# Four weight loads moved up in SyncE's queue, and the second context's split moved ahead of a small transpose's reading

## The chip, the cores and the metric

The kernel runs on one core of a Trainium2 chip. The metric is device microseconds for one execution of the whole program, lower is better. TensorE (PE) multiplies, VectorE (DVE), ScalarE (ACT) and GpSimd (POOL) do the elementwise work, and SyncE (SP) issues all of this kernel's DMAs from one queue. Each engine runs its own instructions in the order in which they were written, and waits on semaphores for the others.

## The reference, cut to what matters

Two cross-attention layers in sequence over 32 batches, 112 queries of 320 channels, 375 context rows of 512, 20 heads of 16. Both layers attend to the same context.

```python
# layer 0: text rows 0..76, image rows 77..374
q = heads(x @ Wq.T)
out  = attend(q, heads(text @ Wk.T), heads(text @ Wv.T))
out += attend(q, heads(ip @ Wk_ip.T), heads(ip @ Wv_ip.T))
x = out @ Wo.T + bo + x
# layer 1: text rows 0..370, image rows 371..374
q = heads(x @ W_q)
probs = softmax(q k_text / 4)
qsem = l2norm(probs @ text_ehs); sem = qsem . l2norm(ip_ehs)
probs_ip = softmax(q k_ip / 4 + 0.5 * sem) * spatial_mask
x = (probs @ v_text + probs_ip @ v_ip) @ W_out + b_out + x
```

## The kernel before, in words

The order of all work is one list of stages, written by hand in `stage_order`. Each engine has a function (`tensor`, `vector`, `scalar`, `gpsimd`, `sync`) that walks the list and issues its own part of each stage; so moving one line of `stage_order` moves work in the queues of all the engines that take part in that stage, and of no others. Stages of 32 batches follow one another with the next batch's projections mixed into the current one's attention; a batch takes some 78 us, and only the first two batches have a start of their own. The change lies in that start.

The start, in the order of the list (b is the batch, l the layer, t text, None a tile that is shared by both layers):

- A context (512 x 375) is loaded by `("ctx", b)` and split by `("split", b)` into a rounded part `ch` (four ACT copies) and a rest `cl` (four POOL subtractions). Context 0 is loaded into `pvt`, context 1 into `w2both`, which the raw weights use before it.
- `keys(b, l, m)` makes one tile of keys: PE multiplies into a bank R, ACT rounds into `kst`, DVE subtracts, ACT or DVE rounds the rest, POOL subtracts once more, and SP stores the three parts in HBM (`k_split`). `keys(0, 0, 0)` is the first image key tile; its store is line 1362. There are five staging buffers at first: tile (0, 1, 1), the eighth, takes the buffer of tile (0, None, 0), the sixth, and its copy on ACT waits until that tile's store has landed.
- `key_weights 1` rounds and splits the layer-1 key weights `wk1` (tile V in the trace, as they are loaded into the space of V1): ACT writes `wkh`, DVE `wkl`. `keys(0, 1, m)` needs both.
- `("load", 2)` are four DMAs of SP: `wk1` (512 KB), `wvip1`, `wv0` and `wvip0` (640 KB each). The third waits for the split of the first key weights, the fourth for the end of `image_keys` on PE.
- `k_stack` and `q_stack` read the stored keys and queries back from HBM in the layout of the attention (tiles Ks and Qs). Part 0 of the keys and all queries are needed for the first `s_max`.
- `image_values`, `weights 2` and `text_values(0)` come between: ACT and DVE make norms and split `wv0`, then PE makes the values of batch 0.
- `s_max` are eight rounds of PE products whose maxima DVE takes. `m_T` turns them back with one transpose of PE (line 692), ACT copies it into `mrem` and `ms`, POOL makes three parts (`m_split`), and SP sends them in six DMAs into rows of Qs (line 1397). These are "the first maxima's turning back". The attention's `scores` wait for these DMAs.
- `("split", 1)` stood behind this. PE's `keys(1, 0, 0)` and `keys(1, 0, 1)`, which need it, stand ahead of the first `scores`.

PE's list around the end of the start is thus: `s_max` x8, `m_T`, two key tiles of batch 1, `scores` 0.

Of the kernel before, what the change touches and what calls it, by code (L numbers as in the profile page):

```python
# [52 lines left out]
def stage_order():  # L53
    o = Order()
# [3 lines left out]
    def in_bank(what, signal, value):  # L58
        o.share("R", 3, what, signal, value)

    def flush():
        now = later[:]
        later.clear()
        for stage in now:
            o.add(*stage)

    def keys(b, l, m):
        o.add("k", b, l, m)
        in_bank(("k", b, l, m), "k_rem", o.at("k", b, l, m))
        o.share("rem", 2, ("k", b, l, m), "k_low", o.at("k", b, l, m))  # L70
# [158 lines left out]
    def take(pieces, n):  # L229
        for _ in range(n):  # L230
            next(pieces, None)
# [11 lines left out]
    o.add("image_keys")  # L243
    for m in range(3):
        in_bank(("image_keys", m), "kip_rem", m + 1)
    keys(0, "t", 1)
    keys(0, 0, 1)
    keys(0, "t", 2)
# [1 line left out]
    keys(0, None, 0)  # L250
    queries(0, 0)
    o.add("key_weights", 1)
    o.add("load", 2)
    o.add("k_stack", 0, 0, 0)
    o.add("k_stack", 0, 0, 1)
    o.add("q_stack", 0, 0)
# [20 lines left out]
    rows0 = maxima(0, 0, lambda: take(start, 1))  # L277
    take(start, 99)
    flush()
    take(rows0, 9)  # L280
    o.add("split", 1)
    o.add("weights", 1)
    o.add("weights_done")
    rows1 = iter(())
# [97 lines left out]
def xattn_two_layers(nc, a, out):  # L382
# [3 lines left out]
    with ctx:  # L386
# [6 lines left out]
        def sem(name):  # L393
# [121 lines left out]
                                             "ones_rows", "wvip0", "wo0", "wq1", "wo1", "wv1", "small")}  # L515

        o = stage_order()
        at, slot = o.at, o.slot

# [976 lines left out]
```

## Time and profile before

| | us |
|---|---|
| median of 3 runs | 2602.32 (2602.14 to 2607.59) |
| the profiled execution | 2602.31 |
| its span from first to last instruction | 2600.5 |
| PE busy | 2466.5 (95%) |
| DVE busy | 1640.2 (63%) |
| ACT busy | 1233.1 (47%) |
| POOL busy | 767.3 (30%) |
| mean granted clock of TensorE | 0.984 |

The busy time is from the profile's page; PE being busy does not mean that it works at its peak. The timeline lists instructions in order of time; the waits tell what ended the idle time of each engine; the DMA view gives the time from a DMA's issue to its landing.

### The profile page before, as it was taken

To read this page: it belongs to the slowest core of one execution; us is meant where nothing else is said; L and a number is where in the kernel's file an instruction comes from. 1 tells how busy PE (TensorE), PEld (TensorE's weight loads), DVE (VectorE), ACT (ScalarE), POOL (GpSimd) and SP (SyncE) were. 2 spreads that over 40 slices of the span, in tenths; PEclk is the share of its full clock that TensorE was granted. 3 is DMA by queue.
4 is the path that set the end of the run, shared out by engine and by line. 5 is a ranking of instruction groups with operands and counts; after the bars stand their busy time and mean duration, and the time that the engine had idled before them with its cause. 6 is when DMAs were issued, how large, how long until landed. Compare 5 with 4: busy or idle time off the path is not lost.

```text
span 2600.5 us, 64042 instructions
## 1 busy us (share of the span) xinstructions
PE 2466.5 (95%) x26280; PEld 2120.9 (82%) x26280; DVE 1640.2 (63%) x3210; ACT 1233.1 (47%) x2305; POOL 767.3 (30%) x999
## 2 busy tenths in 40 slices
PE   4799999999999999999999999999999999999996
PEld 4688888888888888888888888888888888888874
DVE  2356676566676566676656676656676656667655
ACT  2344444554444554444554444554444554444543
POOL 2122323322333332332332332332332332333222
PEclk8899999999999999999999999999999999999997
DMA  7664767656677656677655577745677755567730
GB/s 184 119 98 80 105 96 105 86 91 93 89 95 105 98 84 89 89 95 114 89 87 88 86 108 100 100 75 92 95 94 104 94 85 90 85 93 98 89 38 7
DMA packets 493225, 241.46 MB, mean 93 GB/s; under 512 B 259627, under 2 KB 492923, under 8 KB 492924
## 3 DMA queue, kind: packets, MB, share of 16 engines
q1 hardware_dynamic: 492934, 237.37, 61.7%
q8 instruction: 208, 3.41, 0.7%
q14 instruction: 83, 0.68, 0.1%
HBM read 171.35 MB, written 64.59 MB: 91 GB/s over the span
## 4 chain that ended last, share of the span: by engine, by line
PE 78%; DVE 17%; issue 2%; ACT 1%; DMA 1%; SPq 1%; POOL 0%; DVEq 0%; ACTq 0%; POOLq 0%
PE ST L701 7%; DVE w L838 6%; PE PN L718 5%; PE R L745 5%; PE R L643 5%; PE R L657 4%; PE R L656 4%; PE R L594 4%; DVE m L922 4%; PE R L595 4%; PE PN L763 3%; PE R L659 3%; PE R L802 3%; PE R L597 3%; DVE w L835 3%; PE ST L683 2%
## 5 line engine op out<-in xcount | busy, mean ns | idle before, releaser
L1141 ACT ACTIVATE p<-ST 128x1344 f32<-128x1344 f32 x320 | 413.8, 1293 | 113.1 <-PE ST L704 108.7
L1271 POOL TENSOR_TENSOR w<-w 128x448 f32<-128x448 f32 (+1 forms) x256 | 331.0, 1293 | 424.9 <-DVE w L835 406.7
L838 DVE SCALAR_TENSOR_TENSOR w<-p,pr 128x1344 f32<-128x1344 f32 x160 | 296.7, 1854 | 174.7 <-ACT pr L1156 161.5
L835 DVE TENSOR_TENSOR rem<-R,kst 128x298 f32<-128x298 f32 (+2 forms) x181 | 89.9, 497 | 441.4 <-ACT kst L1035 441.4
L745 PE MATMUL R<-pr,Gh 128*128 128x448 f32 (+1 forms) x960 | 366.7, 382 | 0.0
L835 DVE TENSOR_TENSOR w<-R,w 128x448 f32<-128x448 f32 (+1 forms) x480 | 281.5, 620 | 70.5 <-PE R L750 60.1
L656 PE MATMUL R<-wvh,ch 128*128 128x320 f32 (+3 forms) x896 | 301.9, 337 | 3.7 <-DVE wvl L835 3.7
L1204 POOL TENSOR_TENSOR kst<-rem,kst 128x298 bf16<-128x298 f32 (+2 forms) x181 | 149.2, 824 | 480.4 <-ACT kst L1035 260.2
L657 PE MATMUL R<-wvh,cl 128*128 128x320 f32 (+3 forms) x896 | 279.1, 311 | 0.0
L594 PE MATMUL R<-ch,wkh 128*128 128x298 f32 (+1 forms) x640 | 217.2, 339 | 27.1 <-DVE wkl L835 21.7
L701 PE MATMUL ST<-Qs,Ks 100*128 100x112 bf16 (+1 forms) x3520 | 229.8, 214 | 13.1 <-DMA Qs<-ms 5.2
L701 PEld LDWEIGHTS ST<-Qs,Ks 100*128 100x128 bf16 (+1 forms) x3520 | 184.7, 98 | 65.9 <-issue 34.8
L1035 ACT ACTIVATE pvt<-PN 128x112 f32<-128x112 f32 (+1 forms) x320 | 98.0, 306 | 250.2 <-PE PN L767 193.4
L659 PE MATMUL R<-wvl,ch 128*128 128x320 f32 (+3 forms) x672 | 209.2, 311 | 0.0
L1156 ACT ACTIVATE pr<-ST 128x1344 fp32r<-128x1344 f32 x160 | 204.9, 1281 | 0.0
L595 PE MATMUL R<-cl,wkh 128*128 128x298 f32 (+1 forms) x640 | 202.1, 316 | 0.0
L745 PEld LDWEIGHTS R<-pr,Gh 128*128 128x128 f32 (+1 forms) x960 | 176.5, 184 | 22.6 <-issue 6.2
L748 PE MATMUL R<-pr,Gl 128*115 128x448 f32 (+1 forms) x480 | 176.3, 367 | 0.0
L750 PE MATMUL R<-pr,Gl 128*128 128x448 f32 (+1 forms) x480 | 175.8, 366 | 0.0
L926 DVE TENSOR_REDUCE m<-ST 112x3 f32<-112x1113 f32 x128 | 167.9, 1312 | 7.2 <-PE ST L685 7.2
L1035 ACT ACTIVATE V<-R 128x320 f32<-128x320 f32 (+2 forms) x160 | 67.5, 437 | 218.6 <-PE R L660 218.6
L656 PEld LDWEIGHTS R<-wvh,ch 128*128 128x128 f32 (+3 forms) x896 | 162.5, 181 | 9.0 <-issue 4.1
(189 smaller groups left out, 5825.6 us busy)
## 6 DMA issues: line engine op xcount, KB each, us to landing
Ks<-k_split SPq DMA_DIRECT2D x384, 140.6 KB, 6.0
Ks<-k_split SPq DMA_DIRECT2D x384, 93.8 KB, 8.4
Qs<-q_split SPq DMA_DIRECT2D x384, 70.0 KB, 8.7
w<-in_ctxT SPq DMA_DIRECT2D x31, 750.0 KB, 5.9
k_split<-kst SPq DMA_DIRECT2D x64, 281.2 KB, 3.5
k_split<-kst SPq DMA_DIRECT2D x63, 223.5 KB, 2.7
q_split<-qst SPq DMA_DIRECT2D x128, 84.0 KB, 2.7
k_split<-kst SPq DMA_DIRECT2D x64, 111.8 KB, 2.5
```

Of the source, the lines that this page charges most:

```text
L594: e.matmul(r[:, 0:t1 - t0], wh[:, k, c0:c0 + 128], h[:, k, t0:t1], start=k == 0, stop=False)
L595: e.matmul(r[:, 0:t1 - t0], wh[:, k, c0:c0 + 128], lo[:, k, t0:t1], start=False, stop=False)
L656: e.matmul(r[0:n, 0:C], h[:, k, :], wh[:, k, :], start=k == 0, stop=False)
L657: e.matmul(r[0:n, 0:C], lo[:, k, :], wh[:, k, :], start=False, stop=False)
L659: e.matmul(r[0:n, 0:C], h[:, k, :], wl[:, k, :], start=False, stop=False)
L701: e.matmul(ST[:, u, S * h:S * h + S], Ks[l][0:m, GH * g + h, 128 * u:128 * u + 128], Qs[l][0:m, GH * g + h, :], start=True, stop=True)
L745: e.matmul(r[0:nj, 0:QW], Gh[0:ROWS[u], q:q + nj], x[0:ROWS[u], QW * u:QW * u + QW], start=u == 0, stop=False)
L835: return e.tensor_tensor(to, x, y, op)
L838: return e.scalar_tensor_tensor(out=to, in0=x, scalar=s, in1=y, op0=op0, op1=op1)
L1141: e.activation(p32[i][:].rearrange("p (u q) -> p u q", u=3), st, ACT.Exp).then_inc(p_whole, 1)
L1156: e.activation(pr[n % 2][:].rearrange("p (u q) -> p u q", u=3), ST[:, :, 0:QW], ACT.Exp).then_inc(p_round, 1)
L1271: e.tensor_tensor(first, first, w2[n % 2][0:ROWS[j], QW * j:QW * j + QW], ALU.add).then_inc(ns_added, 1)
```

## The change

In `stage_order`, `("load", 2)` moves from behind `key_weights 1` to directly behind the stage `image_keys`. On SP, the only engine with a part in it, the four loads then stand behind the store of the first image key tile. And `("split", 1)` moves ahead of the remaining steps of `rows0` (`m_T` and `m_split`).

```diff
     for m in range(3):
         in_bank(("image_keys", m), "kip_rem", m + 1)
+    o.add("load", 2)
     keys(0, "t", 1)
...
     o.add("key_weights", 1)
-    o.add("load", 2)
     o.add("k_stack", 0, 0, 0)
...
     flush()
+    o.add("split", 1)
     take(rows0, 9)
-    o.add("split", 1)
     o.add("weights", 1)
```

SP's queue at the start. Each row is one DMA, written tile<-source tile; V is `wk1`'s place, p_1, w and p_0 those of the other three weights. Both pieces, where the loads stand now and where they stood:

```order
 L1362 DMA k_split<-kst 128x3x298
+L1286 DMA V<-in_wk 128x4x256
+L1286 DMA p_1<-in_wvip 128x4x320
+L1286 DMA w<-in_wv 128x4x320
+L1286 DMA p_0<-in_wvip 128x4x320
 L1357 DMA k_split<-pvt 128x3x77 x4
 L1362 DMA k_split<-pvt 128x3x298
```

```order
 L1379 DMA q_split<-qst 128x3x112 x2
 L1379 DMA q_split<-qst 64x3x112
-L1286 DMA V<-in_wk 128x4x256
-L1286 DMA p_1<-in_wvip 128x4x320
-L1286 DMA w<-in_wv 128x4x320
-L1286 DMA p_0<-in_wvip 128x4x320
 L1372 DMA Ks<-k_split 16x12x375 x6
 L1372 DMA Ks<-k_split 16x8x375 x6
```

They have moved past 19 DMAs: 15 stores of keys (lines 1357 and 1362), the load of the next text context (tx), and the three stores of the queries.

ACT's queue around the turning back (V is a copy of batch 0's values, `ch` the rounded context 1):

```order
 L1035 ACTIVATE V<-R 119x20x16
-L1035 ACTIVATE mrem<-R 40x112
-L1035 ACTIVATE ms<-R 40x112
-L1035 ACTIVATE ch<-w 128x375 x4
+L1035 ACTIVATE ch<-w 128x375 x4
+L1035 ACTIVATE mrem<-R 40x112
+L1035 ACTIVATE ms<-R 40x112
 L1035 ACTIVATE wvh<-p_1 128x1280
```

POOL's queue at the same place:

```order
-L1204 TENSOR_TENSOR mrem<-mrem,ms 40x112
-L1260 CAST ms<-mrem 40x112
-L1204 TENSOR_TENSOR ms<-mrem,ms 40x112
-L1204 TENSOR_TENSOR cl<-w,ch 128x375 x4
+L1204 TENSOR_TENSOR cl<-w,ch 128x375 x4
+L1204 TENSOR_TENSOR mrem<-mrem,ms 40x112
+L1260 CAST ms<-mrem 40x112
+L1204 TENSOR_TENSOR ms<-mrem,ms 40x112
 L1228 MEMSET V 128x60
```

The rows of the split and of the turning back have changed places on both engines. PE and DVE have the same instructions in the same order as before.

## Rows read from the trace of the kernel before

**Rows 1.** Timeline of SyncE's queue: start, duration (us), line, DMA; each row one or several.

```profile
21.88 0.36 SPq L1362 DMA_DIRECT2D k_split<-kst  x1
...
26.98 2.79 SPq L1357 DMA_DIRECT2D k_split<-pvt  x4
...
36.61 1.23 SPq L1362 DMA_DIRECT2D k_split<-kst  x2
...
39.90 0.63 SPq L1286 DMA_DIRECT2D V<-in_wk  x1
...
42.73 0.91 SPq L1286 DMA_DIRECT2D p<-in_wvip  x1
44.08 8.00 SPq L1372 DMA_DIRECT2D Ks<-k_split  x12
52.12 8.05 SPq L1387 DMA_DIRECT2D Qs<-q_split  x6
...
64.89 0.43 SPq L1304 DMA_DIRECT2D w<-in_ctxT  x1
```

**Rows 2.** Timeline around PE's longest gap; brackets: idle time before, and its releaser.

```profile
46.52 1.06 ACT L1035 ACTIVATE wkh<-V 128x1024 fp32r<-128x1024 f32 x1 [14.07 <-DMA V<-in_wk]
...
48.89 0.68 PE L594 MATMUL R<-ch,wkh 128*128 128x372 f32 x1 [16.93 <-DVE wkl L835]
```

**Rows 3.** DMA issues: KB each, median us from issue to landing, of single stretches.

```profile
V<-in_wk SPq DMA_DIRECT2D x1, 512.0 KB, 6.6
...
k_split<-kst SPq DMA_DIRECT2D x1, 111.8 KB, 7.5
...
Qs<-q_split SPq DMA_DIRECT2D x2, 70.0 KB, 5.4
...
w<-in_ctxT SPq DMA_DIRECT2D x1, 750.0 KB, 9.7
```

**Rows 4.** Stretches: five engines' busy us, granted TensorE clock, mean DMA busy share, GB/s.

```profile
24.00:26.00 2.00, 2.00 (x15) 1.86 (x14) 0.57 (x2) 0.79 (x2) 0.00 (x0) 1.00 0.00 0
...
38.00:40.00 2.00, 0.00 (x0) 0.00 (x0) 0.00 (x0) 0.00 (x0) 0.00 (x0) 0.50 0.78 150
...
46.00:48.00 2.00, 0.00 (x0) 0.00 (x0) 0.39 (x1) 1.06 (x1) 0.00 (x0) 0.50 1.07 376
```

**Rows 5.** Timeline from the eighth key tile's copy to the first maxima.

```profile
55.54 0.48 ACT L1035 ACTIVATE kst<-R 128x371 bf16<-128x371 f32 x1 [0.92 <-PE R L598]
...
62.75 0.52 PE L656 MATMUL R<-wvh,ch 128*77 128x320 f32 x1 [3.75 <-DVE wvl L835]
...
70.24 0.48 PE L683 MATMUL ST<-Ks,Qs 96*112 96x375 bf16 x2
```

**Rows 6.** The same stage one batch later: the stacks' issue and the maxima that need them.

```profile
111.12 6.37 SPq L1372 DMA_DIRECT2D Ks<-k_split  x12
...
117.53 5.23 SPq L1387 DMA_DIRECT2D Qs<-q_split  x6
...
128.05 0.50 PE L683 MATMUL ST<-Ks,Qs 96*112 96x375 bf16 x2 [3.08 <-DMA Qs<-q_split]
```

**Rows 7.** Timeline of the turning back, the second split and the first scores.

```profile
81.13 0.35 PE L692 MATMUL R<-ident_sb,m 112*40 112x112 f32 x1 [1.73 <-DVE m L922]
81.51 0.26 ACT L1035 ACTIVATE mrem<-R 40x112 f32<-40x112 f32 x1 [8.37 <-PE R L692]
...
82.06 0.39 POOL L1204 TENSOR_TENSOR mrem<-mrem,ms 40x112 f32<-40x112 f32 x1 [23.45 <-ACT ms L1035]
...
83.22 3.51 POOL L1204 TENSOR_TENSOR cl<-w,ch 128x375 fp32r<-128x375 f32 x4
83.28 5.13 SPq L1397 DMA_DIRECT2D Qs<-ms  x6
...
86.83 0.59 PE L594 MATMUL R<-ch,wkh 128*128 128x298 f32 x1 [5.36 <-POOL cl L1204]
...
92.29 0.71 PE L701 MATMUL ST<-Qs,Ks 102*128 102x112 bf16 x11
```

## The prediction, made before the changed kernel was run

> **What bounds the kernel now.** The table of busy time comes first: PE is busy in 95% of the span, so an edit of the start can only pay through gaps of PE there, and what it saves there should reach the end whole, since nothing afterwards goes by an absolute time. The timeline of the first 93 us shows the gaps. The largest is 16.9 us: PE ends the queries of batch 0 at 31.97 and starts key tile (0, 1, 0) at 48.89, released by DVE's `wkl` [rows 2]. Followed back: `wkl` follows ACT's `wkh` of 46.52, and ACT had waited 14.07 us for the load of `wk1` [rows 2]. That load was issued at 39.90 only, behind the stores, and landed 6.6 us later [rows 1, 3]. The second gap is 5.4 us: after the transpose `m_T` at 81.13, PE waits until 86.83 for POOL's `cl` of context 1, which POOL began only after the three steps of `m_split` [rows 7]. Then the first scores run at 92.29, with no wait of their own [rows 7].
>
> **Part 1, the four loads.** On SP: the first image key store ends at 22.24, and the next store starts at 26.98 because its tile is ready only then [rows 1]. The loads took 39.90 to 43.64, that is 3.74 us to issue [rows 1]; from 22.3 they end at 26.0, 1.0 us before that store. So the move costs SP's queue nothing; without that cover the price would be 3.7 us for every store behind. The DMA engines were idle at 24 to 26 [rows 4], so `wk1` lands at about 22.3 + 6.6 = 28.9, before ACT wants it. ACT had last worked at 32.45, 14.07 before `wkh`; from `wkh` to PE's key tile it took 48.89 - 46.52 = 2.37 us [rows 2]. With the queries' own steps on DVE beside it, the tile starts at about 35.0 in place of 48.89. That looks like 13.9 us, but it does not all arrive.
>
> What is late next? First, the eighth key tile's copy on ACT waits for the landing of the sixth tile's store. It was issued at 36.61 and took 7.5 us, so it landed at about 44.1, and SP's first `k_stack` at 44.08 had waited for it as well [rows 1, 3]. In the new order the tx load and query stores still surround it, but no weight load comes after it, so 44.1 is the upper bound for the copy, T. The lower one is PE's: its two key tiles took 6.6 us at the slow clock, 48.89 to the copy at 55.54 [rows 2, 5], and from 35.0 they end at 41.6. I take T = 43, the middle, since the row shows the landing next to traffic that mostly stays. From that copy to the values on PE it took 62.75 - 55.54 = 7.2 us, and from there to the first maxima 70.24 - 62.75 = 7.5 us [rows 5]. So PE is at the maxima at 43 + 14.7 = 57.7 by its own work.
>
> Second, the maxima need the stacks. Before, these were issued from 44.08 to 60.17, the last landed 5.4 us after an issue at about 59.3, at 64.7, and nobody waited: the maxima came at 70.24 [rows 1, 3, 5]. That took 20.6 us with the DMA engines full (share 1.07, 376 GB/s at 46 to 48) [rows 4]; at that rate the 2.49 MB of weights were 6.6 us of it. One batch later, without such loads, it took from 111.12 to 128.05, 16.9 us, and there PE did wait [rows 6]. So the bounds are 14.0 (20.6 less 6.6) and 16.9 us after T. I take 16.5, nearer to the measured row: the maxima start at 59.5. **PE's gap of 17 us becomes three smaller ones**, and this stage is 10.7 us earlier, not 13.9.
>
> The clock: it fell to the lower of its two levels in the gap (0.50 at 38 to 40) [rows 4], and it may now fall between 57 and 60 instead, which puts values tile 2 in the midst of the maxima at half speed. I charge 0.7 us for the sweep of 10.9 us (70.24 to 81.13), which DVE mostly paces. `m_T` is then at 59.5 + 10.9 + 0.7 = 71.1, 10.0 earlier.
>
> **Part 2, the split.** `cl` becomes ready without waiting for the turning back, if context 1 is there. Its load was issued at 64.89 and landed 9.7 us later, 74.6 [rows 1, 3], 6.5 us ahead of `m_T`; that was slack. ACT stood idle 8.37 us before `mrem` [rows 7], so ahead of it the four copies (1.7 us) are free only as long as the context lands some 2 us before `m_T`. Now the context comes behind the stacks. SP: the stacks take 11.6 us (6.37 and 5.23) as a batch later [rows 6], from T = 43 to 54.6; the stretch from 60.17 to the context's issue at 64.89 (4.7 us) follows; issue at 59.3, landing 9.7 later at **69.0** (67 to 73). ACT's copies end at 70.8. POOL's `cl` ran 3.51 us [rows 7] and starts 0.5 behind the first copy: 69.5 to 73.0. `m_split` on POOL would start at 72.0 (0.93 after `m_T`, as from 81.13 to 82.06 [rows 7]) and now starts at 73.0: **1 us lost on this path**, 1.2 with the handover. The three steps took 1.2 us, 82.06 to 83.2, so they end at 74.2.
>
> PE: the two key tiles start when `cl` is done, 73.0, and take 5.46 us (86.83 to 92.29) [rows 7]: 78.5. The scores also wait for the six DMAs of `ms`: issue 5.13 us [rows 7], 79.4, and a landing for which the trace has no row. It is bounded by 0 and by 92.29 - 88.41 = 3.9 us, since the scores then ran without waiting. I take 2, the middle. So the scores start at 81.4: **the turning back's DMAs, not `cl`, now end last**. That is 92.29 - 81.4 = 10.9 us earlier. Part 2 alone would have saved only 92.29 - 90.4 = 1.9 us of PE's 5.4, since those DMAs come to 90.4 there.
>
> PE now idles 2.9 us ahead of the scores, where before it came from 5.5 us of work and had just got its clock back. I charge 0.9 us for slow first products (the 5.46 us of key tiles lost at most half of that to the low clock, and behind the scores PE waits for ACT anyway). After that all follows at its old distance. **Sum: 10.7 - 0.7 + 0.9 = 10.9; less 0.9 = 10.0 us.** Span 2590.5; the profiled execution, 2602.31, was 1.8 above its span and equals the median 2602.32, so the time is 2592.3.
>
> The engines' order of service, by rule: the Trainium skill, "DMA: Bandwidth & Descriptors", section "Queues, rings and completion order", states that each DMA engine consumes the descriptors of a queue's ring in ring order. All of this kernel's DMAs are on one queue, so the text key stores issued from 26.98 would stand behind 2.49 MB of weights. The trace agrees as far as it goes: the sixth tile's store, issued right behind a 616 KB load, took 7.5 us where the last query stack, with nothing big ahead, took 5.4 [rows 3]. The rule is weighed as rival B.
>
> **Rivals.**
> B, the stacks come late: stores behind the loads push T out. The four loads take an estimated 12.5 us in all, 2.8 until the last is issued and then its landing, at most the 9.7 us of the larger context [rows 1, 3]; from 22.3 they are through by 35. Even at 38 to 40 the DMA engines had room (share 0.78) [rows 4], so a backlog of some 3 to 4 us at 35 should be worked off by 41, and T stays. If it isn't, T is 46 to 47: the maxima at 63, gain 6.5 us, 2595.8. Against it: the idle share at 24 to 26 [rows 4].
> C, context 1 lands late: at 73 to 74 instead of 69, the landing of before less the little that SP gains. ACT's `mrem` and `ms` are now queued behind the copies that wait for it, POOL's `m_split` behind `cl`, and SP's six DMAs behind that. `cl` ends at 77.5, `m_split` at 78.7, scores at 85.9: gain 6.4, less 0.9, 5.5: 2596.8.
> D, the gain does not reach the end: batch 1's maxima wait for its query stack (3.08 us) [rows 6], on a chain of stores and stacks that starts in batch 0. If DMA work displaced from the start meets it, most is given back: gain 0 to 4, 2600.
> E, slower: the same queue as C, but deciding. Context 1 would have to land after 80 us (`cl` 4 us later, `m_split` 1.2, DMAs 7.1 make 92.3), and for a measurable loss after 85. It landed at 74.6 with all loads ahead of it, and no work is added ahead of it, so only a much worse service of the DMA engines does this: 2608.
>
> **How the numbers follow.** Forecast (A, 2588.5 to 2594.5) 0.66; B 0.12; C 0.12; D 0.06; E 0.04. About 0.2%, 5.2 us, is what a measurement of this kernel can tell from no change; faster means below 2597.1. A, most of B, half of C and a little of D give 0.80; the rest of these 0.16; E 0.04. The bounds in A: T 41.6 or 44.1 moves the time by -1.4 or +1.1, stacks 14.0 by -1.8 (PE's own work then decides), stacks 16.9 +0.4, the context's landing -1.2 or +3, the landing of `ms` -2 or +1.9, the clock -1 or +2. The range reaches from 2588.5 over A, B, C to 2598.5.
>
> **What would show it.** In the trace of after: SP's loads at 22.3 to 26.0 and the text store still at about 27; ACT's `wkh` at 32.5; PE's key tile at about 35; the eighth tile's copy released by a DMA at about 43; the first maxima waiting for Qs at about 59.5, which refutes me if they start below 57 or above 62; `cl` ahead of `mrem`; PE idle ahead of the first scores at about 81.4, released by the DMAs of `ms`. What makes it wrong: a store stream that the loads hold up, or context 1 later than `m_T`.

## The result, and the profile after

The changed kernel took 2599.35 us (median of 20 runs, 2593.22 to 2608.21), the kernel before 2604.99 us (20 runs, 2596.65 to 2608.52). The ratio is 0.9982 with a 95% interval of 0.9975 to 0.9989: 4.7 us faster (2.9 to 6.5 by the interval), where 10.0 had been forecast. The direction was right, the size was less than half, and the time lies outside the range of 2588.5 to 2598.5. The median of before had been 2602.32 in the three runs at hand; with 20 runs it is 2.7 us higher. Medians here are over all executions, ratios leave out those in a slow state (one each of e5, e8 and e9 below), and the one trace taken in such an execution is e9's (3412.1 us at a mean granted clock of 0.652).

The first trace of the changed kernel (its execution took 2608.21 us, the slowest of the 20) misleads if read alone. So a second trace of the same kernel was taken (e12, 2598.1 us span), and both are shown. SyncE's queue in the first trace, columns as in [rows 1]:

```profile
21.89 0.36 SPq L1362 DMA_DIRECT2D k_split<-kst  x1
22.30 0.49 SPq L1286 DMA_DIRECT2D V<-in_wk  x1
...
23.99 1.07 SPq L1286 DMA_DIRECT2D p<-in_wvip  x1
...
26.89 6.04 SPq L1357 DMA_DIRECT2D k_split<-pvt  x4
...
32.97 1.26 SPq L1362 DMA_DIRECT2D k_split<-pvt  x1
...
34.27 5.73 SPq L1357 DMA_DIRECT2D k_split<-pvt  x8
...
40.68 1.23 SPq L1362 DMA_DIRECT2D k_split<-kst  x2
...
48.27 5.59 SPq L1372 DMA_DIRECT2D Ks<-k_split  x12
```

The loads are issued from 22.30 to 25.06, a little faster than forecast, and the first text store is on time at 26.89. But then the issuing itself slows: four stores take 6.04 us where they took 2.79 [rows 1], and the 13 stores of the text side (tile pvt) as a whole 13.1 us in place of 8.9. The sixth tile's store comes at 40.68 (36.61 before) and the stack at 48.27 (44.08 before). The same queue in the second trace:

```profile
27.99 2.80 SPq L1357 DMA_DIRECT2D k_split<-pvt  x4
30.83 1.15 SPq L1362 DMA_DIRECT2D k_split<-pvt  x1
32.03 6.85 SPq L1357 DMA_DIRECT2D k_split<-pvt  x8
...
39.56 1.23 SPq L1362 DMA_DIRECT2D k_split<-kst  x2
...
46.97 5.59 SPq L1372 DMA_DIRECT2D Ks<-k_split  x12
```

Here the first text store starts 1.1 us later than in the first trace, the delay sits in later stores, and the 13 take 10.9 us. What followed on the other engines, second trace (compare [rows 2, 5, 7]):

```profile
33.36 1.05 ACT L1035 ACTIVATE wkh<-V 128x1024 fp32r<-128x1024 f32 x1
...
47.41 0.48 ACT L1035 ACTIVATE kst<-R 128x371 bf16<-128x371 f32 x1 [6.28 <-DMA k_split<-kst]
...
55.45 0.52 PE L656 MATMUL R<-wvh,ch 128*77 128x320 f32 x1 [3.67 <-DVE wvl L835]
...
64.02 0.50 PE L683 MATMUL ST<-Ks,Qs 96*112 96x375 bf16 x2 [1.29 <-DMA Qs<-q_split]
...
74.06 1.73 ACT L1035 ACTIVATE ch<-w 128x375 fp32r<-128x375 f32 x4 [7.16 <-DMA w<-in_ctxT]
...
74.72 3.52 POOL L1204 TENSOR_TENSOR cl<-w,ch 128x375 fp32r<-128x375 f32 x4 [24.25 <-ACT ch L1035]
...
75.14 0.35 PE L692 MATMUL R<-ident_sb,m 112*40 112x112 f32 x1 [1.86 <-DVE m L922]
...
78.19 1.65 POOL L1204 TENSOR_TENSOR mrem<-mrem,ms 40x112 f32<-40x112 f32 x1
...
80.67 5.13 SPq L1397 DMA_DIRECT2D Qs<-ms  x6
...
86.98 1.21 PE L701 MATMUL ST<-Qs,Ks 102*128 102x112 bf16 x11 [2.88 <-DMA Qs<-ms]
```

ACT waits 6.28 us for the sixth tile's store: the wait the forecast called T, at 47.4 in place of 43. The maxima wait for the query stack and start at 64.02 (70.24 before). Context 1 lands at 74.0, only 1.1 us ahead of `m_T`, so POOL is still at `cl` when `ms` is ready. The first scores wait for the DMAs of `ms` and start at 86.98: 5.3 us earlier than before. In the first trace the maxima start at 67.12, `m_T` at 79.97 and the scores at 90.42, only 1.9 us earlier than before.

The next difference lies in batch 1. From batch 0's transposes of x (line 811) to batch 1's it took 67.8 us before, 75.1 in the first trace and 70.4 in the second. In both, PE waits longer for the query stack of batch 1 than the 3.08 us of [rows 6]; the rows are from the first and the second trace:

```profile
129.71 0.84 PE L683 MATMUL ST<-Ks,Qs 96*112 96x375 bf16 x2 [6.03 <-DMA Qs<-q_split]
```

```profile
125.77 0.84 PE L683 MATMUL ST<-Ks,Qs 96*112 96x375 bf16 x2 [5.66 <-DMA Qs<-q_split]
```

So of the 5.3 us gained at the scores in the second trace 2.3 are left at batch 1's first maxima (128.05 before), and its span is 2.4 us shorter. Behind batch 1 these traces lie parallel: from its transposes of x to those of batch 30 it takes 2248.6 us before, 2248.8 and 2249.2 in the two traces.

### The profile page after: what moved, and what is told of

It reads as the page before. It is cut to its first block, busy times and chain, and to the rows that moved or that the text cites. A ratio compares the mean times of both kernels' runs of the same rounds, so it can differ in the third digit from the quotient of the medians.

```text
span 2606.4 us, 64042 instructions
## 1 busy us (share of the span) xinstructions
PE 2474.0 (95%) x26280; PEld 2125.6 (82%) x26280; DVE 1638.1 (63%) x3210; ACT 1233.3 (47%) x2305; POOL 768.7 (29%) x999
## 4 chain that ended last, share of the span: by engine, by line
PE 77%; DVE 17%; SPq 2%; issue 2%; DMA 1%; ACT 1%; POOL 0%; DVEq 0%; ACTq 0%; POOLq 0%
PE ST L701 7%; DVE w L838 6%; PE PN L718 5%; PE R L745 5%; PE R L643 5%; PE R L657 4%; PE R L656 4%; PE R L594 4%; DVE m L922 4%; PE R L595 4%; PE PN L763 3%; PE R L802 3%; PE R L659 3%; PE R L597 3%; DVE w L835 3%; PE ST L683 2%
## 6 DMA issues: line engine op xcount, KB each, us to landing
Ks<-k_split SPq DMA_DIRECT2D x384, 140.6 KB, 6.0
```

## The experiments

Each kernel is compared with the kernel before on the same chip. The table's stage times are from one trace each, and traces of one kernel differ (see e12); "13 stores" is SyncE's time from the first to the end of the last text-side key store (tile pvt).

| kernel | median (runs) | ratio, 95% interval | 13 stores | stack | maxima | scores |
|---|---|---|---|---|---|---|
| before | 2604.99 (20) | | 8.9 | 44.1 | 70.2 | 92.3 |
| after, first trace | 2599.35 (20) | 0.9982 (0.9975 to 0.9989) | 13.1 | 48.3 | 67.1 | 90.4 |
| e12, after again | 2600.39 (12) | 0.9985 (0.9975 to 0.9995) | 10.9 | 47.0 | 64.0 | 87.0 |
| e1, four loads only | 2602.67 (12) | 0.9995 (0.9986 to 1.0004) | 12.3 | 48.4 | 67.1 | 91.6 |
| e2, split only | 2602.14 (12) | 0.9992 (0.9983 to 1.0) | 9.0 | 45.2 | 72.3 | 91.4 |
| e3, one load | 2600.62 (11) | 0.9981 (0.9972 to 0.999) | 9.0 | 45.3 | 64.9 | 86.9 |
| e4, one load and split | 2600.23 (12) | 0.9989 (0.9979 to 1.0) | 8.9 | 44.0 | 63.8 | 86.4 |
| e5, two loads | 2597.22 (8) | 0.9966 (0.9955 to 0.9977) | 8.9 | 45.6 | 61.2 | 82.9 |
| e6, e4 and text context late | 2595.04 (6) | 0.9964 (0.9951 to 0.9977) | 8.9 | 42.3 | 62.5 | 83.9 |
| e7, e6 and context 1 first | 2592.69 (6) | 0.9953 (0.9941 to 0.9965) | 8.9 | 42.3 | 62.6 | 81.7 |
| e8, after and a fill on PE | 2604.72 (12) | 0.9998 (0.999 to 1.0007) | 10.6 | 47.6 | 65.8 | 88.6 |
| e9, three loads | 2596.05 (7) | 0.9963 (0.9949 to 0.9977) | | | | |
| e10, after and both of e7 | 2596.91 (7) | 0.9968 (0.9957 to 0.9979) | 11.4 | 46.4 | 63.8 | 84.7 |
| e11, two loads, split, both | 2589.45 (6) | 0.9947 (0.993 to 0.9964) | 8.9 | 45.0 | 60.9 | 80.4 |

### e1: the loads alone

```diff
     for m in range(3):
         in_bank(("image_keys", m), "kip_rem", m + 1)
+    o.add("load", 2)
...
     o.add("key_weights", 1)
-    o.add("load", 2)
```

> All four loads behind the first image key store, the split left where it was before. My theory now (P): the text stores queued behind the loads hold up SyncE's issuing, so four stores that took 2.79 us to issue take about 6, and the first key stack is issued at about 48.3 instead of 44.1; the first maxima start at about 67 (70.24 before), m_T at about 80. Then m_split comes first, cl about 86, the first scores at about 91.3. Time about 2 to 3 us below before. Rival (Q): the split's new place holds up the stacks or the context; then without it the stack is issued at 43 and the first maxima start at about 60, time 8 to 10 us below before.

The stack came at 48.4, the maxima at 67.1, `m_T` at 79.9, the scores at 91.6. P held in each stage, with 4.73 us for the four stores where about 6 had been expected; Q (that the split holds up the stack) fell.

```profile
26.95 4.73 SPq L1357 DMA_DIRECT2D k_split<-pvt  x4
31.73 1.76 SPq L1362 DMA_DIRECT2D k_split<-pvt  x1
33.53 5.74 SPq L1357 DMA_DIRECT2D k_split<-pvt  x8
```

The DMAs follow one another with 0.05 us between them, so SyncE does not stand waiting for a tile: it is the issuing of each DMA that grows. By itself this part moved the time by less than can be told (0.9995, interval across 1), where 2 to 3 us had been expected.

### e2: the split alone

```diff
     flush()
+    o.add("split", 1)
     take(rows0, 9)
-    o.add("split", 1)
```

> The split ahead of the turning back, the loads where they were before. P: context 1 lands at 74.6, ahead of m_T at 81.1, so ACT's and POOL's copies hide in their idle time; m_split ends at 83.3 as before, its DMAs at about 88.4 and land 1.2 us later, the first scores start at 89.6, 2.7 us earlier. The time falls by 2.7 us. Q (the split is what costs): the scores start at 92 or later, and the time does not fall.

The copies did hide; the split ran from 75.84 on ACT, long before `m_T`:

```profile
75.84 1.73 ACT L1035 ACTIVATE ch<-w 128x375 fp32r<-128x375 f32 x4 [0.59 <-DMA w<-in_ctxT]
...
76.50 3.52 POOL L1204 TENSOR_TENSOR cl<-w,ch 128x375 fp32r<-128x375 f32 x4 [16.06 <-ACT ch L1035]
...
82.96 0.35 PE L692 MATMUL R<-ident_sb,m 112*40 112x112 f32 x1 [1.46 <-DVE m L922]
...
85.05 5.13 SPq L1397 DMA_DIRECT2D Qs<-ms  x6
```

This trace is 1.8 us behind that of before at `m_T` (82.96 against 81.13), for reasons that lie ahead of the edit. From `m_T` to the scores it took 8.4 us in place of 11.2, so 2.8 gained, against 2.7 expected. The median was 2.3 us lower; the interval just reaches 1.

### e3, e5 and e9: how many loads are moved

```diff
     for m in range(3):
         in_bank(("image_keys", m), "kip_rem", m + 1)
+    o.add("load", 5)
...
-                    elif key[0] == 2:
+                    elif key[0] == 5:
                         load("wk1")
+                    elif key[0] == 2:
                         load("wvip1")
```

The line `elif key[0] == 2:` stands one load lower in e5 and two lower in e9.

> Only the first of the four loads (512 KB) moved up; the other three and the split where they were before. P: 0.5 MB in front does not fill the queue, so the four text stores take under 4 us to issue, the first key stack is issued at 43.5 to 44.5, PE's key tile starts at about 34.7, the first maxima at 64.6 (when the last query stack landed before). 5 us earlier than before at the maxima, time 4 to 6 us below before, more than with all four loads. Q (any load ahead of the stores holds SyncE, whatever its size): four stores take 5 us or more, the stack comes at 47 or later, time no better than with all four.

> The first two of the four loads (1.15 MB) moved up, all else as before. P (the bytes ahead of the stores fill the queue and hold up SyncE): between one load (four text stores 3.1 us to issue, stack at 45.3, maxima at 64.9) and four (4.7 to 6.0 us, stack at 48.3, maxima at 67.1): stores about 4 us, stack at about 46, maxima at about 65.5; time 3 to 4 us below before. Q (the number of bytes does not matter, only whether wvip0 waits on PE): as with one load.

> The first three of the four loads (1.8 MB) moved up, wvip0 left at its old place, else as before. So far: no load ahead 2.8 us for the four text stores and the stack at 44.1, one 3.1 and 45.3, two 2.0 and 45.5, four 4.7 and 6.0 and 48.3. P: the hold-up begins between two and four; with three the stores take 3 to 5 us and the stack comes at 46 to 47. A second reading (R): the last query stack lands late in the four-load kernels because no load stands ahead of the stack's DMAs (they then landed 1.34 us apart, against 0.87 to 0.92 with loads ahead); with wvip0 still ahead of them they should land at most 1.0 us apart, and the last query stack 16 to 17 us after the stack's start; without R it takes 18.7 as in after. Time by P 3 to 5 us, with R 5 to 7 us below before.

With one load the 13 stores took 9.0 us, with two 8.9: no hold-up of the issuing. SyncE's rows of e5 (lines are some further down in these kernels):

```profile
27.11 1.97 SPq L1359 DMA_DIRECT2D k_split<-pvt  x4
29.12 0.52 SPq L1364 DMA_DIRECT2D k_split<-pvt  x1
30.77 5.27 SPq L1359 DMA_DIRECT2D k_split<-pvt  x8
```

P had put e5 in between, which is wrong: the issuing is free up to some point and then gets dear. In e3 the stack came 0.8 us later than expected, the maxima at 64.9 as expected. In e5 the maxima came at 61.2, 4 us earlier than either reading had it, as the stacks took only 15.4 us. Two loads are not free, though: in e5 the sixth tile's store landed 8.8 us after its issue (7.5 before), so its stack came at 45.6.

Whether three loads pass the point is open. Their time (9.6 us below before by the ratio) speaks for no large hold-up. So do the rows of e9's one trace, with the reserve that its text stores started 2 us later than e5's, when one of the loads was about to land:

```profile
29.13 1.98 SPq L1359 DMA_DIRECT2D k_split<-pvt  x4
...
34.51 5.27 SPq L1359 DMA_DIRECT2D k_split<-pvt  x8
```

Q of e5 (it matters only whether the fourth load, `wvip0`, is among them) is thereby not refuted: no run has four loads' bytes in front without it. The traces only show that its wait for PE is not what holds SyncE, as it was issued at 23.99, right behind the third. The gains: one load 4.9 us, two 8.9, three 9.6, four 1.3, by the ratios.

### e4: one load and the split

The edits of e3 and e2 together.

> Only the first load moved up, and the split ahead. P: the sum of the two: first maxima at 64.6, m_T at 75.5 to 77; context 1 is issued at about 64.9 as before and lands at 74.6, so cl is done at 78.6 and m_split at 79.8 at the latest, the scores start at 86.5; 5.8 us earlier than before. Time 5 to 7 us below before, the best of the four. Q: at least 2 us less, because the context lands later than m_T.

The scores started at 86.4 as expected, but e3 without the split had them at 86.9, and e4's `m_T` had come 1.1 us earlier (74.53 against 75.65). From `m_T` to the scores it took 11.9 us in e4 and 11.2 in e3 and before: by these single traces the split's place gained nothing here and may have cost 0.7 us, where it had gained 2.8 in e2. The trace shows why (lines are one further down in this kernel):

```profile
73.45 1.74 ACT L1036 ACTIVATE ch<-w 128x375 fp32r<-128x375 f32 x4 [6.76 <-DMA w<-in_ctxT]
...
74.11 3.52 POOL L1205 TENSOR_TENSOR cl<-w,ch 128x375 fp32r<-128x375 f32 x4 [26.70 <-ACT ch L1036]
...
74.53 0.35 PE L693 MATMUL R<-ident_sb,m 112*40 112x112 f32 x1 [1.58 <-DVE m L923]
...
77.59 1.65 POOL L1205 TENSOR_TENSOR mrem<-mrem,ms 40x112 f32<-40x112 f32 x1
```

Context 1 lands 1.1 us before `m_T`; `mrem` on POOL starts 3.1 us behind `m_T` (0.93 before) and takes 1.65 us in place of 0.39. This is rival C at work: with the context this late, the split gives back all that it brings. P's time, 5 to 7 us below before and the best of the four, was missed: the ratio gives 2.9 us, and e3's 4.9. The medians of e3 and e4 are alike (2600.6 and 2600.2).

### e6 and e7: what the landing of the sixth tile's store and of context 1 are worth

e6 is e4 with the first edit, e7 has both.

```diff
-    o.add("text_ctx", QUAD)
     keys(0, None, 0)
...
     o.add("load", 4)
+    o.add("text_ctx", QUAD)
```

```diff
+    o.add("ctx", 1)
     o.add("load", 3)
...
-    o.add("ctx", 1)
```

> wk1 alone moved up and the split ahead, and in addition the load of the next text context (616 KB) moved from in front of the sixth key tile's store to behind the last start loads. P: the stack waits for the landing of that store, which took 7.5 us because of the queue in front of it; without the text context the landing takes 5 to 6 us and the issue is 0.65 us earlier, so the stack starts at 41.5 to 42.5, the maxima at 61 to 62, context 1 lands at 71 to 72, the scores start at 84 to 85; time 7 to 8 us below before. Q (the landing time is latency of its own): landing 7 us or more, stack at 43.5.

> As the one with the late text context, and context 1 is issued ahead of the loads wo0, wq1, wo1 and xn. P: the context's landing (73.4 in e4) came 1 us before m_T, so cl and m_split waited; issued 3 us earlier and without 1.6 MB in front it lands at about 67, cl hides wholly, m_split starts right behind m_T, the scores start 2 us earlier than without this, at 82 to 83; time 8 to 10 us below before. Q (POOL's split was hidden anyway): same time as e6.

Without the text context in front, the two DMAs of the sixth tile's store landed after 4.4 and 5.1 us in place of 7.2 and 6.8 in e4. The stack started at 42.3, as P said, and now right behind SyncE's own loads, with that landing (41.7) past; the maxima at 62.5 came half a microsecond late. The medians fell to 2595.0 and 2592.7. In e7 context 1 landed at 65.8 (71.0 in e6), POOL's `cl` ended at 70.0, ahead of `m_T` at 73.3, and `m_split`'s DMAs were issued at 75.4 (77.5 in e6). The scores came 2.2 us earlier, and the median 2.4 us. By the traces Q fell for both: T and the context's landing are what the start hangs on. By the times it fell for e6; those of e6 and e7, six runs each, lie too close to be told apart (their intervals overlap).

### e10 and e11: the same two edits with four loads, and with two

e10 is the changed kernel with both edits; e11 is e5 with both and the split.

> The changed kernel, and in addition the next text context behind the start loads and context 1 ahead of wo0, wq1, wo1. P: the hold-up of the text stores stays (5 to 6 us), but the sixth tile's store lands earlier, the stack starts at 45.5 to 46.5 (48.3 in after), context 1 lands ahead of m_T, m_T comes at 78, the scores start at 87 to 88 (90.4): 2 to 3 us below the changed kernel. By R the stack's DMAs still land 1.3 us apart, which keeps it well behind the kernel with one load early (scores at 81.7).

> All that helped so far: two loads early, the split ahead, the next text context behind the start loads, context 1 ahead of wo0, wq1, wo1. The stack at about 42.5, its end 16 us later, the maxima at 59 to 60, the scores at 79 to 80; time 11 to 13 us below before, the fastest of all. If two loads early are no better than one, it equals e7 (11 us).

e10: the 13 stores still took 11.4 us and the stack came at 46.4, 4.1 us later than in e7. The scores started at 84.7, 2.3 us ahead of e12; that is better than expected, and still behind e7 by 3.0 us (the ratios, 0.9968 and 0.9953, have intervals that overlap). e11: all stages at or near what was expected but the stack, which came at 45.0 and not 42.5, as the sixth tile's store took 9.2 us to land, with two loads in front of the stores and no text context. Its stack needed only 15.8 us. The ratio 0.9947 is **the fastest kernel of the study, 13.8 us below before** (its interval overlaps those of e5 to e7, e9 and e10).

```profile
26.73 1.98 SPq L1359 DMA_DIRECT2D k_split<-pvt  x4
...
66.48 1.73 ACT L1036 ACTIVATE ch<-w 128x375 fp32r<-128x375 f32 x4 [2.68 <-DMA w<-in_ctxT]
...
67.14 3.52 POOL L1205 TENSOR_TENSOR cl<-w,ch 128x375 fp32r<-128x375 f32 x4 [18.85 <-ACT ch L1036]
...
71.95 0.35 PE L693 MATMUL R<-ident_sb,m 112*40 112x112 f32 x1 [1.86 <-DVE m L923]
72.33 0.26 ACT L1036 ACTIVATE mrem<-R 40x112 f32<-40x112 f32 x1 [4.12 <-PE R L693]
...
72.81 0.39 POOL L1205 TENSOR_TENSOR mrem<-mrem,ms 40x112 f32<-40x112 f32 x1 [2.16 <-ACT ms L1036]
...
74.04 5.13 SPq L1399 DMA_DIRECT2D Qs<-ms  x6
...
80.36 0.71 PE L702 MATMUL ST<-Qs,Ks 102*128 102x112 bf16 x11 [1.24 <-DMA Qs<-ms]
```

Here the split hides as it was meant to: `cl` ends 1.3 us before `m_T`, ACT and POOL wait for PE, and `mrem` takes its 0.39 us.

### e8 and e12: the slow batch 1

e12 is the changed kernel again. e8 adds work that changes no result:

```diff
+                    if key == (1, 0, 0, True):
+                        free(w, "ST", ("s_max", b, l, h0))
+                        for _ in range(30):
+                            e.matmul(ST[:, 0, 0:384], wkh[0][:, 0, 0:128], wkh[0][:, 0, 0:384], start=True, stop=True)
                     w.wait_ge(d_kr[l][0 if h0 + n <= HALVES[0][1] else 1], 96 * (b + 1))
```

> The changed kernel, and 30 products whose result is overwritten (into the bank of the maxima, operands are resident weights) ahead of PE's wait for batch 1's query stack, which was 6.0 us in the trace of after. My theory on the clock (C): the way from the first scores to batch 1's second transposes took 97.4 us with 3.4 us at the low clock between 120 and 160, 105.2 with 13.6 us; the fill keeps the clock up, so that this way takes 96 to 98 us, the low stretches near 129 and 146 are gone, and the median is 2 to 4 us below the changed kernel's (2595 to 2597). Rival (D): the stack's landing, not the clock, sets that way; then the median does not move, or rises by the fill.

> The changed kernel once more, unchanged, for a second trace and more times. C': the trace of after was an unlucky one in batch 1 (75.07 us between the second and the first transposes of x, against 67.8 to 69.6 in the other traces), so this trace has 68 to 71 us there with the same start (stack at 48.3, maxima at 67, scores at 90.4), and its span is 2597 to 2600. D': batch 1 is slow in this order by its nature; then 74 to 76 again. Median 4 to 6 us below before either way.

e12 speaks for C' against D': batch 1 took 70.4 us, the span was 2598.1, the median 2600.4. It is one more trace, and the expectation had left out two: batch 1 took 74.1 us in e5's trace and 66.8 in e7's, so a slow batch 1 is not an accident of one trace only. The stack and maxima came 1.3 and 3 us earlier than I had expected of a repeat, so the start itself also varies by that much between executions of one kernel. Stretches of batch 1, columns as in [rows 4], in the first trace of after (the clock of before was 0.88 and 1.00 in the first two) and then in e8:

```profile
130.00:140.00 10.00, 10.00 (x48) 9.09 (x47) 5.85 (x12) 1.05 (x4) 0.00 (x0) 0.72 1.19 137
140.00:150.00 10.00, 7.01 (x35) 5.13 (x34) 7.37 (x14) 1.35 (x6) 1.05 (x3) 0.79 0.76 136
```

```profile
120.00:130.00 10.00, 10.00 (x69) 9.59 (x67) 3.32 (x6) 0.74 (x2) 0.83 (x1) 1.00 1.25 134
130.00:140.00 10.00, 8.85 (x55) 7.37 (x54) 8.29 (x17) 1.78 (x9) 0.00 (x0) 1.00 0.99 184
140.00:150.00 10.00, 9.03 (x52) 8.41 (x52) 6.93 (x14) 2.73 (x9) 3.50 (x6) 0.83 0.21 62
```

In the first trace of after, PE waited 6.0 us for the query stack of batch 1, until 129.7 (3.1 before), and it ran at the lower of the clock's two levels from 128.8 to 135.6 and from 145.9 to 152.7. Of the 7.2 us that batch 1 lost there, 2.9 are this wait, and 2.3 and 1.9 the two sweeps of maxima behind it. In the second trace only the wait is longer than before (5.7 us); the sweeps are not.

The fill of e8 did keep the clock at 1.00 from 120 to 140, and the first sweep took 12.7 us (14.9 in the kernel before, 17.2 in the first trace). But the clock fell in the second sweep instead, which took 12.8 us in place of 11.2 before, and batch 1 as a whole 69.2 us. The fill was also too long: the query stack had landed at 125.8, and the maxima started at 126.96, behind the fill. The median did not fall: 2604.7, level with before and above after's. So C holds for where that one trace lost its time, and fails as a way to gain any; D was nearer for the time. Why e8 is above after is open: in its trace one batch in mid-run took 80.2 us in place of 78.0, which is too little to explain a median.

## Why the prediction was wrong, point by point

**The sum, term by term** (us; T is the issue of the first key stack):

| | forecast | first trace | second trace |
|---|---|---|---|
| T | 43.0 | 48.27 | 46.97 |
| stack to maxima | 16.5 | 18.85 | 17.05 |
| sweep of maxima, to `m_T` | 11.6 | 12.85 | 11.12 |
| `m_T` to scores | 10.3 | 10.45 | 11.84 |
| scores | 81.4 | 90.42 | 86.98 |

**What bounds the kernel.** Right in that PE's gaps decide, and that a gain once made is kept from batch 2 on. Wrong in that it should reach the end whole; see "To the end".

**Part 1, the queue.** Wrong, and this is the step that failed: "So the move costs SP's queue nothing". The cover for the four issues was there: in the first trace they ended at 25.1, and the next store began at 26.9. But I priced only the issuing of the moved loads, not what they do to the issuing of the stores behind them. These took 10.6 to 13.1 us in the five traces with four loads in front, and 8.9 to 9.0 in the eight with none, one or two. The rows of before held a hint that I passed over: the stacks' own issuing, right behind the loads, took 8.00 and 8.05 us [rows 1], against 6.37 and 5.23 a batch later [rows 6].

**T.** Forecast 43, bounds 41.6 and 44.1. ACT's copy came at 49.0 and 47.4, the stack at 48.3 and 47.0. The stores' hold-up is 4.2 and 2.0 us of that, and in the second trace 1.0 us more is that the text stores started late. The rest is that the sixth tile's store landed after 7.1 to 7.6 us as before, where I had counted on 6.4 because no weights came after it. e6 shows what had made it long: without the text context in front of it, its DMAs take 4.4 and 5.1 us. So the outcome of rival B, given 0.12, is what happened, up to 2 us beyond its own T of 46 to 47. Its mechanism was near but not the same: B had the DMA engines serve the stores late. The early stores did land late (the first after 7.7 and 6.3 us, 3.0 before, with the last load through at 37.1 and 36.1 where B had 35), but by the sixth tile's store the landing time was that of before, and what remained was SyncE's own delay. The comparison that the prediction made for the ring order was weak, too: the last query stack had not "nothing big ahead" but 17 DMAs of the stacks; the last of the key stack landed at 61.8, 2.5 us after the issue of that query DMA.

**The stacks.** 16.5 us from the stack's issue to the maxima; measured 18.9 and 17.0. Taking the weights' bytes from in front of the stacks brought less than by their size (20.5 us from the stack's issue to the last landing with them before, 18.7 and 16.9 without, against 14.0 by their size).

**The clock.** The sweep was charged 0.7 us on top of 10.9 and took 2.0 and 0.2 more, at mean granted clocks of 0.64 and 0.75 (0.85 before). Behind the scores I charged 0.9 us; up to batch 0's transposes of x it was 0.6 and 0.5 (30.1 and 30.0 us in place of 29.6, at 0.94 and 0.95).

**Part 2.** The context's landing was put at 69.0, and was 77.5 and 74.0, since it hangs on the same queue. The margin ahead of `m_T` was 2.5 and 1.1 us, where before it had been 6.6; so rival C came in with B. POOL's three steps ended 4.1 and 5.5 us behind `m_T`, in place of the 3.1 forecast and the 2.1 of before. 1.2 us of this I had not seen at all: `mrem` took 1.65 us (second trace) and the cast 1.46 us (first trace) where they take 0.39 and 0.27, while DVE subtracted for `wvl` beside them. The Trainium skill, "SBUF — State Buffer", section "SBUF: two separate sides", says that a VectorE instruction with two inputs from SBUF and a GpSimd instruction that reads SBUF exclude each other for a whole instruction. The trace agrees: before, the same subtraction met `cl` and took 3.35 us, here 1.49 to 2.28, and POOL's step beside it got long.

What the split's place is worth goes by that margin. From `m_T` to the scores it took 10.7 to 11.7 us in the four traces with the split behind (before, e1, e3, e5). With the split ahead it took 8.4 us where the context landed 5.5 us or more before `m_T` (e2, e7, e10, e11), 10.1 to 10.6 at 2.2 to 2.8 us (first trace, e6, e8), and 11.8 to 11.9 at 1.1 us (e4, second trace).

**What ends last ahead of the scores.** Right: the DMAs of `ms`, with PE waiting 2.4 and 2.9 us. Their landing takes 1.2 us after the last issue, I had taken 2.

**To the end.** "After that all follows at its old distance" put the way from the scores to the end at nothing but the clock's 0.9 us, and that failed as well. From the scores to batch 1's first maxima both traces lost 3.5 and 3.0 us against before, where PE waits for the query stack of batch 1 (6.03 and 5.66 us in place of 3.08). This is the wait that rival D, given 0.06, had named. Ten of the twelve traces of changed orders (e9's left aside) have lost 1.1 to 3.5 us there, e7's and e11's nothing. e2's lost 3.4 although no load was moved in it, so what makes that stack late is open. In the second trace 5.3 us at the scores became 2.4 at the end of the span. The ratios of many executions give 4.7 and 3.9 us; the trace of before is of an execution 2.7 us below its median.

**The range.** It had room for B alone or C alone, and for a base of 2602.3. Both came together, as they share a cause, part of D came on top, and the base was 2.7 us low.

## What to carry to other kernels

A transfer moved up in a queue of DMAs has two prices: its own issuing, and the slower issuing of what is behind it once enough stands in front of it. Read the second from the issue times of DMAs that stand behind large ones, and move only as much as the work in the gap needs. Here two of the four loads cost nothing in issuing and 1.3 us in a later landing (e5); four cost 2 to 4 us in issuing. Where two rivals hang on one queue, give them a joint chance and let the range hold both. A step that is moved ahead of a wait on a transfer (here the split ahead of `m_T`) pays only once that transfer is early enough: e4 gained nothing by it, e2 gained 2.8 us, and in e11 it was hidden whole.

## What the runs showed of the hardware

- SyncE's issuing of small-row stores grew from 0.49 us each to 1.0 to 2.3 us for several in a row with 2.49 MB of loads in front of them. With none or 0.5 MB in front one of the first four took 1.2 to 1.7 us, with 1.15 MB none did. The durations are of the issuing itself, back to back. What causes it, and from how many bytes or DMAs on, was not tried.
- The stack's first five DMAs landed on average 1.2 to 1.35 us apart in the five traces where all four loads were early, and 0.8 to 1.1 us apart in the others that have loads in front of them, for the same 140.6 KB each. The stretch of 50 to 58 us of after and of e3, columns as in [rows 4]:

```profile
50.00:58.00 8.00, 2.97 (x12) 2.67 (x13) 5.29 (x10) 3.76 (x4) 1.41 (x2) 0.50 1.17 110
```

```profile
50.00:58.00 8.00, 3.79 (x16) 2.86 (x15) 3.88 (x6) 4.35 (x5) 0.00 (x0) 0.71 1.16 168
```

The DMA engines are as busy in both and move 110 or 168 GB/s. Reading R had predicted at most 1.0 us for e9, and the last query stack 16 to 17 us after the stack's start. Its trace has 1.05 us and 14.6 us, which is nearer to R than to the 18.7 us without it, and is one trace only. Why larger transfers ahead should make the small ones behind them faster is open.
- The executions of one and the same kernel differ by 15 us (after) and 12 us (before) in 20 runs. Two traces of one kernel show it in the start (3.4 us at the scores) and in batch 1 (4.7 us), almost none of it (0.4 us) in the 29 batches after. Over all traces but e9's those 29 batches took 2248.6 to 2252.7 us. For a change of 5 us one trace shows where, and only many times show how much.
